# The first pass of a two-block transformer kernel with its stages in another order on the five engines

## What is computed

```python
xn = _layernorm(x)
# block 0: causal attention, 32 heads of 8, 8 key/value heads, rotary; output projection
scores = jnp.einsum('bhqd,bhkd->bhqk', q, k_rep) / scale
scores = jnp.where((kpos > qpos)[None, None], -jnp.inf, scores)
out = jnp.einsum('bhqk,bhkd->bhqd', jax.nn.softmax(scores, axis=-1), v_rep)
# beside it: gelu(x8 @ w_gating[0]) * (x8 @ w_gating[1]) -> @ w_linear, inputs rounded to fp8
# both are added to x
# block 1: layernorm; rotary attention in which the 16 heads of ONE token attend to each other
scores = jnp.einsum('bshd,bstd->bsht', q, k) / jnp.sqrt(jnp.float32(HD))
# beside it: silu(gate) * up with ternary-quantized weights, rms norm, @ ternary w_proj
# both are added to x
```

## Time and profile before

| | before |
|---|---|
| median of 3 runs | 570.97 us (569.65 to 571.83) |
| span of the profiled execution | 569.0 us |
| PE busy | 521.8 us, 92% of the span |
| ACT busy | 468.1 us, 82% |
| DVE busy | 394.9 us, 69% |
| POOL busy | 236.9 us, 42% |

### The profile page before, as it was taken

One profiled execution on the slowest core, in us unless ns is written; L12 is line 12 of the kernel. 1 busy time (PEld: TensorE's weight loads), 2 busy tenths in 40 slices (PEclk: granted clock), 3 DMA queues, 4 the chain that ended last, 5 costly groups with the idle time before them and its releaser, 6 DMA issues.

```text
span 569.0 us, 12415 instructions
## 1 busy us (share of the span) xinstructions
PE 521.8 (92%) x4660; PEld 257.6 (45%) x4705; DVE 394.9 (69%) x845; ACT 468.1 (82%) x607; POOL 236.9 (42%) x302
## 2 busy tenths in 40 slices
PE   3288899999999999999999999999999999998795
PEld 1142334333444655545544444564444453455564
DVE  4587999878687588676787875755553546667583
ACT  2199999999999999999988898978898888873441
POOL 4466947533536225243966633252332230250100
PEclk9569999999999999999999999999999999999898
DMA  8913302221452633414234554364435026158853
GB/s 273 277 25 93 99 14 57 51 21 33 52 104 41 104 58 49 97 37 52 58 56 75 83 91 73 53 109 72 86 100 62 17 75 112 40 68 154 120 118 81
DMA packets 214397, 46.06 MB, mean 81 GB/s; under 512 B 197440, under 2 KB 213056, under 8 KB 214336
## 3 DMA queue, kind: packets, MB, share of 16 engines
q1 hardware_dynamic: 213760, 44.93, 40.9%
q10 hardware_dynamic: 576, 0.33, 0.3%
HBM read 19.02 MB, written 10.49 MB: 52 GB/s over the span
## 4 chain that ended last, share of the span: by engine, by line
PE 71%; DVE 6%; DMA 5%; SPq 5%; issue 5%; POOL 4%; ACT 4%; DVEq 0%; POOLq 0%; ACTq 0%
PE psV L706 20%; PE psS L692 7%; PE psS L828 3%; PE psB L875 3%; PE psC L875 3%; PE psC L782 2%; PE psA L875 2%; PE psB L782 2%; ACT Pt L958 2%; PE psC L743 2%; PE psA L885 2%; DMA stage<-in_wg 2%; PE psB L885 2%; SPq L509 1%; POOL Pt L1633 1%
## 5 line engine op out<-in xcount | busy, mean ns | idle before, releaser
L958 ACT ACTIVATE Pt<-psS 128x1024 f32<-128x1024 f32 x288 | 279.9, 1030 | 26.3 <-PE psS L692 23.8
L706 PE MATMUL psV<-Pt,vaug 128*32 128x512 f32 x1152 | 151.4, 604 | 2.9 <-POOL Pt L1633 2.3
L1633 POOL TENSOR_SCALAR_AFFINE_SELECT Pt<-Pt 128x1024 f32<-128x1024 f32 x64 | 72.3, 1156 | 77.3 <-ACT Pt L958 77.1
L692 PE MATMUL psS<-qTf,kTf 32*128 32x512 f16 x576 | 65.1, 388 | 2.9 <-ACT Pt L958 2.2
L692 PEld LDWEIGHTS psS<-qTf,kTf 32*128 32x128 f16 x576 | 17.6, 91 | 84.4 <-ACT Pt L958 47.7
L706 PEld LDWEIGHTS psV<-Pt,vaug 128*32 128x32 f32 x1152 | 24.3, 108 | 43.7 <-issue 35.5
L1016 ACT ACTIVATE stage<-psS 128x1024 f32<-128x1024 f32 x32 | 31.0, 1022 | 9.1 <-PE psS L828 9.0
L1613 POOL TENSOR_TENSOR rt<-qkv,cs 128x320 f32<-128x320 f32 x16 | 16.7, 1046 | 50.4 <-DVE qkv L1189 26.1
L1624 POOL TENSOR_TENSOR QXf<-rt,QXf 128x512 f16<-128x512 f32 x16 | 19.2, 1200 | 43.0 <-ACT QXf L945 43.0
L1683 POOL TENSOR_TENSOR ss<-ss,mhalf 128x1 f32<-128x1 f32 x16 | 9.7, 607 | 61.9 <-DVE ss L1470 61.9
L1313 DVE SCALAR_TENSOR_TENSOR ga<-gw,gb 128x512 bf16<-128x512 f32 x32 | 23.2, 726 | 5.1 <-ACT gw L984 5.0
(11 more groups left out here) (354 smaller groups left out, 1138.6 us busy)
## 6 DMA issues: line engine op xcount, KB each, us to landing
qkvscr<-rqkv SPq DMA_DIRECT2D x16, 384.0 KB, 2.9
G<-qkvscr SPq DMA_DIRECT2D x24, 128.0 KB, 3.8
stage<-in_wg SPq DMA_DIRECT2D x4, 512.0 KB, 8.9
w8g<-qkvscr SPq DMA_DIRECT2D x16, 128.0 KB, 3.7
oscr<-o SPq DMA_DIRECT2D x16, 128.0 KB, 3.0
at<-oscr SPq DMA_DIRECT2D x16, 128.0 KB, 2.2
out<-yout SPq DMA_DIRECT2D x16, 128.0 KB, 2.3
x<-in_x SPq DMA_DIRECT2D x1, 1536.0 KB, 12.2
```

The costliest lines, as they stand in the source:

```text
L692: e.matmul(psS[j], kd[32 * j:32 * j + k, h, 128 * at:128 * at + 128], qd[32 * j:32 * j + k, 4 * h:4 * h + 4, :].rearrange("p s n -> p (s n ...
L706: ins = e.matmul(psV[32 * j:32 * j + 32, :], vaug[:, at, j, 32 * h:32 * h + 32], Pt[(4 * Q + j) % NP], start=(kb == 0 and h == 0), stop=(k ...
L958: e.activation(flat(Pt4[:, u % NP:u % NP + 2, :]), flat(psS4[:, j:j + 2, :]), ACT.Exp, scale=scale).then_inc(S["exp"], 1)
L1633: e.affine_select(out=p, in_=p, pattern=[[0, 8], [1, 128]], compare_op=ALU.is_ge, fill=0.0, base=0, channel_multiplier=-1).then_inc(S["mas ...
```

## The change

The five strings of `ORDER` are replaced. Each new list holds exactly the same stage names as the old one (711 on PE, 421 on ACT, 628 on DVE, 146 on POOL, 152 on SP); every function stands as it was. The first and last lines of the lists, as far as they are spoken of below; between them the lists differ in many places, by a few positions each:

```diff
     "pe": (
-        "xnT.0 qkv.0 ts.0 xnT.1 qkv.1 up.0 up.1 ts.1 qk.0 up.2 xnT.2 up.3 qk.1 qkv.2 pv.0 qk.2 td.0 up.4 up.5 pv.1 qk.3 "
-        "pv.2 qk.4 pv.3 qk.5 xnT.3 obT.0 up.6 pv.4 td.1 qk.6 pv.5 qk.7 qkv.3 tr.0 pv.6 qk.8 tr.1 xnT.4 pv.7 qk.9 up.7 "
...
+        "xnT.0 xnT.1 ts.0 qkv.0 qkv.1 xnT.2 ts.1 qkv.2 up.0 qk.0 td.0 qk.1 xnT.3 tr.0 up.1 td.1 qk.2 pv.0 up.2 pv.1 "
+        "up.3 qk.3 pv.2 qk.4 up.4 obT.0 pv.3 qk.5 qkv.3 pv.4 qk.6 attT.0 pv.5 qk.7 up.5 pv.6 qk.8 pv.7 obT.1 tr.1 qk.9 "
...
     "act": (
-        "tc.0 qh.0 wh.0 g.0 sq.0 qh.1 fh.0 exp.0 g.1 sin.0 sq.1 exp.1 fh.1 exp.2 tde.0 th.0 exp.3 qh.2 exp.4 g.2 fh.2 "
...
+        "tc.0 qh.0 sin.0 wh.0 g.0 qh.1 exp.0 sq.0 tde.0 exp.1 tde.1 fh.0 th.0 exp.2 g.1 fh.1 exp.3 qh.2 exp.4 g.2 exp.5 "
...
     "dve": (
-        "vz.0 ln0.0 xn.0 xnTc.0 ln0.1 w8.0 qkvc.0 xn.1 ln0.2 w8.1 xnTc.1 ln0.3 idc.0 w8.2 q0.0 va.0 wide.0 kl.0 qkvc.1 "
-        "w8.3 tsc.0 tab.0 q0.1 xn.2 wide.1 va.1 tsc.1 tm.0 ln0.4 xnTc.2 tcs.0 qkvc.2 kl.1 cst.0 ge1.0 ob.0 xn.3 ge3.0 "
...
-        "rng.0 hx.14 osum.14 yout.13 hh.30 sg.31 o1r.15 hh.31 o1.15 ssm.15 at1Tc.14 hx.15 yo.14 at1Tc.15 yout.14 "
-        "osum.15 rngb.0 yo.15 yout.15 fl.0"),
+        "vz.0 ln0.0 idc.0 xn.0 ln0.1 ln0.2 xn.1 xnTc.0 xn.2 w8.0 xnTc.1 tab.0 qkvc.0 va.0 tsc.0 wide.0 xnTc.2 tsc.1 "
+        "w8.1 q0.0 qkvc.1 kl.0 ln0.3 w8.2 wide.1 w8.3 va.1 q0.1 tm.0 tcs.0 xn.3 qkvc.2 kl.1 xnTc.3 tw.0 wide.2 ge1.0 "
...
+        "yout.13 hh.30 osum.14 sg.31 o1r.15 hh.31 o1.15 ssm.15 at1Tc.14 hx.15 yo.14 yout.14 osum.15 at1Tc.15 yo.15 "
+        "rngb.0 yout.15 fl.0"),
     "pool": (
-        "zero.0 rs0.0 gz.0 rs0.1 rope.0 rs0.2 ql.0 rope.1 rs0.3 ql.1 mask.0 mask.1 rope.2 ql.2 mask.4 mask.5 rs0.4 "
-        "rs0.5 rope.3 ql.3 rs0.6 mask.10 mask.11 xf.0 rope.4 xf.1 ql.4 rs1.0 mask.18 mask.19 rope.5 rs0.7 rs0.8 xf.2 "
...
+        "zero.0 rs0.0 rs0.1 rs0.2 rope.0 ql.0 rope.1 rs0.3 ql.1 mask.0 mask.1 rope.2 rs0.4 ql.2 mask.4 mask.5 rs0.5 "
+        "rope.3 ql.3 mask.10 rs0.6 mask.11 gz.0 rope.4 xf.0 ql.4 xf.1 rs1.0 mask.18 mask.19 rope.5 rs1.1 ql.5 rs0.7 "
...
     "sp": (
-        "wg.2 wg.3 qt.0 kt.0 qt.1 kt.1 wg.4 qt.2 wg.5 kt.2 qt.3 wt.2 kt.3 wt.3 qt.4 wt.4 xt.0 wt.5 kt.4 qt.5 xt.1 vw.0 "
...
-        "at1r.10 vw.12 vr.12 ht.11 xt.14 ow.11 vw.13 at1r.11 vr.13 ht.12 xt.15 vw.14 out.10 ow.12 vr.14 at1r.12 vw.15 "
...
+        "wg.2 wg.3 kt.0 qt.0 qt.1 kt.1 wt.2 qt.2 wg.4 wg.5 kt.2 qt.3 wt.3 qt.4 kt.3 xt.0 qt.5 xt.1 kt.4 wt.4 wt.5 kt.5 "
...
+        "vw.12 ht.11 vr.12 xt.14 vw.13 ow.11 at1r.11 out.9 vr.13 ht.12 xt.15 vw.14 ow.12 vr.14 out.10 at1r.12 out.11 "
```

## The result

| | before | after |
|---|---|---|
| median | 570.31 us (4 runs) | 564.59 us (4 runs) |
| span of the profiled execution | 569.0 us | 562.7 us |
| PE busy | 521.8 us | 518.6 us |
| last `pv` ends | 509.1 us | 503.2 us |

The ratio is 0.9892, 95% interval 0.987 to 0.9915: about 6 us faster (5.7 by the medians, 570.3 x 0.0108 = 6.2 by the ratio), where 3.3 were forecast. A second measurement (experiment 15) gave 0.9894, 0.9881 to 0.9907.

The account below looks back on a forecast made before the run. PE was taken to bound 150 to 509 us, leaving the head most to give: 1.6 + 1.7 = 3.3 us, other stretches 0, so the median goes from 570.97 to 567.7 us; 8 in 10 range 563.0 to 572.8.

Parts of the forecast that it names:

- The middle, 150 to 509: Stretch from 150 to 509 us: no gain, between +2 and -1.5 us, as only 3.25 us of PE idle are there.
- The head's sum: First 43 us, up to the start of exp.3: 1.6 + 1.7 = 3.3 us gained.
- the first term: Head, up to the end of up.0: it ends at 27.0 instead of 28.60 us, 1.6 us gained.
- the second term: Head, from up.0 to exp.3 on ACT: the sine and one table load leave the path, 1.7 us gained.
- The load that the prediction left on the path: Head, on ACT: the table load back to the exponential, ahead of exp.0, 1.28 us, still counted.
- The ramp: Stretch from 43 to 150 us: change of 0, bounds -3 and +2.5 us, with gz.0 moved in at no cost.
- Rival B: Ramp: gz.0's memsets lock out DVE there and most of the gain is lost, 570.5 us; chance 0.22.
- the prediction's last sign of being wrong: Whole kernel: the forecast is wrong if exp.3 comes early and the end doesn't.
- The tail: Stretch from 509 to 569 us: change of 0, +-1 us, with the same stages in nearly the same order.
- A: Head: weight piece wg.3 lands late, at 30.0, and up.0 comes 4.9 us later, 572.6 us; chance 0.13.
- C: Ramp: better hand-overs of PE and ACT also take out half of its 8.3 us idle, 563.5 us; chance 0.15.
- D: Bank fills wait for late DVE readers, 0.5 us lost in each of 16 tiles, 575.7 us; chance 0.08.

Follow-up runs that it names:

- experiment 15: The kernel after, unchanged, measured a second time: 564.07 us, 0.9894 of the kernel before.
- 1: New lists up to exp.12 (about 66 us), the rest of each list in the old order: 571.09 us, 1.0008 of the kernel before.
- 4: Old lists up to exp.12, the rest in the new order: 572.08 us, 1.0027 of the kernel before.
- 3: Old lists up to exp.84, the rest in the new order: 571.32 us, 1.0016 of the kernel before.
- 7: Old lists up to 212 us (qk.55), new after it: 570.70 us, 1.0007 of the kernel before.
- 13: Old lists up to exp.143, new after it, so the new tail alone: 570.22 us, 1.0007 of the kernel before.
- 2: New lists up to exp.84 (about 308 us), old after it: 566.19 us, 0.9941 of the kernel before.
- 5: New lists up to 73 us (qk.15), old after it: 572.74 us, 1.0044 of the kernel before.
- 6: New lists up to 212 us (qk.55), old after it: 567.83 us, 0.9944 of the kernel before.
- 8: The kernel after with 11 pairs of pv in PE's list split by the stage behind them: 567.50 us, 0.9940 of the kernel before.
- 9: New lists up to 73 us, old after it, with rope.4 ahead of xf.0 and ql.4 ahead of xf.1 on POOL: 573.13 us, 1.0032 of the kernel before.
- 11: The kernel after with gz.0's five memsets back in the head, behind rs0.0: 564.24 us, 0.9881 of the kernel before.
- 12: The kernel after with seven more pairs of pv side by side in PE's list: 570.30 us, 0.9988 of the kernel before.
- 16: The kernel after with the 13 pairs of pv split that the old list doesn't have: 567.38 us, 0.9946 of the kernel before.
- 10: The kernel after with sin.0 moved from behind qh.0 to behind g.1 on ACT: 567.68 us, 0.9934 of the kernel before.

## Why the prediction was right or wrong

**Wrong at the middle.** The step that failed: "From 150 to 509 us PE is busy 355.75 of 359 us: PE is the bound, and no order of the lists can take more than 3.25 us out of it", and from it "The middle, 150 to 509. 0, between +2 and -1.5". PE was the bound, but its busy time is not fixed by the operations. It depends on which stage stands behind which, 0.2 us for a pair of `pv`. The middle gained 3.0 us (370.6 to 367.6). Between the complete traces of 1 and 4 it is 4.0 us, 2.8 of them in the busy time. The 3.25 us of idle were less room than they seemed, too: run 1, with the old order, idles 1.3 us from 150 to 509 in a trace that lacks no record. That the gain lies near 3.25 is chance.

**The head's sum was right, and by the means both of its terms.** Five profiles with the old lists up to `exp.3` (before, 3, 4, 7, 13) have it at 43.01 to 44.62, mean 43.7; eleven with the new ones (after, 1, 2, 5, 6, 8, 9, 11, 12, 15, 16) at 39.35 to 41.26, mean 40.4. The difference is 3.3 us, as forecast. `up.0` ends at 28.8 in the mean of the five and at 27.2 in the eleven: 1.6 us, the first term. `w8.3` ends 0.8 us earlier and `up.0` starts 0.06 us behind it instead of 0.75, as the prediction had it. From the end of `up.0` to `exp.3` it takes 14.9 and 13.1 us: 1.8, for the second term of 1.7.

Here there was luck in it. The load that the prediction left on the path is nearly hidden (`exp.0` starts 2.46 us behind the end of `up.0`, and 2.20 before), but ACT waits 1.04 us for PE ahead of a `tde`, where the prediction had no wait. And the clock was left out: the earlier trace rows has it at 0.72 over the first 43 us, the kernel after has 0.84 there. How much of the 1.8 us is the order and how much the clock no run separates; put back into the new lists, the sine costs 0.8 us at `exp.3` (10).

By the rule of the Trainium skill ("ScalarE: Activation LUTs", "What ACT_TABLE_LOAD costs") the second term would have been 3.1 us, an estimate from its drain of 1.38 us. The rows show none: in 10 too the sine starts 1.29 us after its load, of 1.28 us, does.

**The ramp: 0, right.** 87.61 us before, 87.71 and 87.72 after, with `gz.0` moved into it. Rival B's place was wrong, but its idea shows in 1, 5 and 9: with the old order behind a new head, all of the head's gain is given back by `exp.30`. That is also the prediction's last sign of being wrong, `exp.3` early and the end not, but it shows in these runs and not in the kernel after.

**The tail: 0, right** (13).

**Rivals.** A fell: `w8.3` shows no wait at 25.66. C, the ramp closing too, is not what happened, though its 563.5 us came near the measured time. D fell with the middle's gain. (B's time is summed wrong by 0.2 us: 570.97 less 0.7 is 570.3.)

## What to carry to other kernels

A busy share of 99 per cent bounds what idle time can be taken out, not what the order can: look up what each pair of neighbours costs on the bound engine (here the same stage took 0.88 us ahead of its like and 1.00 ahead of others) and group like with like, as long as nobody waits longer for it. Price a move off one engine's path also by what the others do meanwhile, and a part of an order is not to be judged alone: cut out and set between old neighbours, the head of a gain of 6 us brought nothing (1) and the rest of it a loss of 1.5 us (4). Before a small idle time is read as room, look whether the trace has all records: the number of weight loads (4705) against that of matmuls (4660) tells it here.

## What the runs showed of the hardware

- Two groups of matmuls of one form (128*32, float32) back to back take 1.92 us and 1.07 + 1.06 apart, with only a short group of another form between them. Which part of the engine pays wasn't tested.
- After 3.82 us of idling, PE was granted half its clock until 47 us, through 3 us in which it was busy without a gap: `pv` took 1.94 us and 1.06 elsewhere. One late stage on ACT cost PE a second time.
- Profiles of one code differ mostly in the head: `exp.3` over 1.9 us in eleven of them. 1.3 us of that are there at the end of `up.0` (26.74 to 28.08), which follows the landing of the weight pieces. The rest goes with the clock: PE was at 0.50 for 8.5 us behind `up.0` in 8, and `exp.3` came 12.62 us behind it; in 1 it was 10.6 us, and 13.56. The other nine lie in order between them. That the clock is the cause is inferred from this order.
- From `exp.3` to `exp.30` seven of the eight profiles with the new lists there (and sine in its new place) agree within 0.03 us, 87.70 to 87.73. The eighth (8), with the same order of PE up to there, was granted 0.50 from 62.6 to 66.0 us and took 88.11. One profile of each kernel would have sized the head's gain at 2.5 us, the mean sized it at 3.3.
